# Another order of the prologue and the first phase in a hand-ordered fp32 attention block

## The reference, cut to what matters

```
x = x + 0.5 * ffn(_layernorm(x))       # ffn: layernorm with gamma, beta; times ternary weight; plus bias
x = x + attn(_layernorm(x))            # 16 query heads, 4 key/value heads, head size 128, rope
x = x + 0.5 * ffn(_layernorm(x))       # the same ffn weights
...
allowed = (j <= i) & (i - j <= WINDOW)                   # WINDOW = 64
weights = softmax(where(allowed, q @ k.T / sqrt(HD), -inf))
...
scale = mean(abs(w)); w_q = clip(round(w / (scale + Q_EPS)), -1, 1)
```

## Time and profile before

| | us |
|---|---|
| median of 3 runs | 791.79 |
| the profiled execution | 793.39 |
| its span, first to last instruction | 790.5 |
| PE busy | 778.3 |
| DVE, ACT, POOL busy | 626.1, 469.6, 455.7 |

### The profile page before, as it was taken

How to read it: one execution, slowest core, us unless ns; L and a number is a source line. 1 busy time by engine, 2 the same in 40 slices (tenths; PEclk the granted TensorE clock), 3 DMA queues, 4 the chain that set the end, 5 groups by cost and what they waited for, 6 DMA issues and landing times.

```text
span 790.5 us, 16087 instructions
## 1 busy us (share of the span) xinstructions
PE 778.3 (98%) x5630; PEld 727.2 (92%) x5630; DVE 626.1 (79%) x1321; ACT 469.6 (59%) x1602; POOL 455.7 (58%) x466
## 2 busy tenths in 40 slices
PE   8999999999999999999999999999999999999997
PEld 7688999999999999999999999999999999999996
DVE  5888967988688877888769887688867988688757
ACT  5366665657646565655747556475664657645574
POOL 3778555766446754567536773476635676446443
PEclk9999999999999999999999999999999999999999
DMA  8572324352252423425153242533224452243410
GB/s 300 114 194 59 90 55 120 95 127 48 55 152 63 121 54 89 126 55 120 41 135 94 68 99 49 134 92 97 67 55 121 94 129 45 57 104 68 107 29 27
DMA packets 54352, 74.10 MB, mean 94 GB/s; under 512 B 7168, under 2 KB 30208, under 8 KB 54272
## 3 DMA queue, kind: packets, MB, share of 16 engines
q1 hardware_dynamic: 53712, 72.74, 37.7%
q10 hardware_dynamic: 560, 0.34, 0.2%
HBM read 14.33 MB, written 4.19 MB: 23 GB/s over the span
## 4 chain that ended last, share of the span: by engine, by line
PE 92%; DVE 3%; POOL 2%; DMA 1%; issue 1%; ACT 0%; SPq 0%; DVEq 0%; POOLq 0%
PE job_p L656 33%; PE attn_p L656 22%; PE scores_p L673 13%; PE heads_p L656 11%; PE probsT_p L737 7%; PE job_p L833 4%; PE job_p L817 2%; POOL q_s L1282 1%; DMA x_res<-wo 1%; POOL probs L1271 1%; DMA x_in<-x 0%; DVE parts L1015 0%; DMA rope_swap<-rope_sin 0%; POOL wo_s L1253 0%; DVE rope_sin L934 0%
## 5 line engine op out<-in xcount | busy, mean ns | idle before, releaser
L656 PE MATMUL attn_p<-wo_s,headsT 128*128 128x256 f32 x1536 | 209.2, 286 | 1.0 <-ACT headsT L1175 0.7
L656 PE MATMUL job_p<-xnT,wq_s 128*128 128x512 f32 x768 | 205.3, 403 | 1.2 <-DVE v_s L951 1.1
L656 PEld LDWEIGHTS attn_p<-wo_s,headsT 128*128 128x128 f32 x1536 | 196.5, 191 | 7.0 <-ACT headsT L1175 1.4
L1154 ACT ACTIVATE probs<-scores_p,neg_max 128x96 f32<-128x96 f32 x512 | 167.6, 352 | 51.8 <-DVE neg_max L900 51.6
L1271 POOL TENSOR_TENSOR probs<-probs,inv_sum 128x384 f32<-128x384 f32 x128 | 107.9, 843 | 152.0 <-DVE inv_sum L906 151.9
L1282 POOL TENSOR_TENSOR q_s<-q_s,rope_swap 128x512 f32<-128x512 f32 x128 | 164.3, 1291 | 52.3 <-DMA rope_swap<-rope_sin 52.2
L1175 ACT ACTIVATE headsT<-heads_p,columns_s 128x512 fp32r<-128x512 f32 x128 | 88.0, 688 | 140.9 <-PE heads_p L656 140.5
L656 PEld LDWEIGHTS job_p<-xnT,wq_s 128*128 128x128 f32 x768 | 135.8, 189 | 26.6 <-DVE v_s L951 1.7
L934 DVE SCALAR_TENSOR_TENSOR rope_sin<-job_p,columns_s,rope_t 128x512 f32<-128x512 f32 x160 | 118.9, 743 | 21.1 <-PE job_p L656 19.9
L673 PE MATMUL scores_p<-k_s,q_s 128*128 128x96 f32 (+2 forms) x1024 | 131.6, 272 | 0.3 <-POOL q_s L1282 0.2
L673 PEld LDWEIGHTS scores_p<-k_s,q_s 128*128 128x128 f32 x1024 | 126.5, 192 | 3.4 <-POOL q_s L1282 1.1
(11 more groups left out here) (96 smaller groups left out, 972.7 us busy)
## 6 DMA issues: line engine op xcount, KB each, us to landing
rope_swap<-rope_sin SPq DMA_DIRECT2D x320, 128.0 KB, 2.3
v_odd<-v_s SPq DMA_DIRECT2D x64, 192.0 KB, 3.3
x_in<-x SPq DMA_DIRECT2D x15, 256.0 KB, 4.2
out<-x_res SPq DMA_DIRECT2D x15, 256.0 KB, 2.5
x_tr<-x_transposed SPq DMA_DIRECT2D x7, 512.0 KB, 5.3
q_s<-wq SPq DMA_DIRECT2D x3, 512.0 KB, 10.1
q_s<-wo SPq DMA_DIRECT2D x2, 512.0 KB, 10.6
x_res<-wo SPq DMA_DIRECT2D x2, 512.0 KB, 4.8
```

Source lines behind the costliest of these rows:

```text
L656: mm = nc.tensor.matmul(dst, a(p), b(q), start=clears and i == 0, stop=len(pairs) == 1, skip_group_check=True)
L1154: ins = nc.scalar.activation(probs[:, i, k, 0:REACH], scores_p[i][:, k, 0:REACH], ACT.Exp, bias=neg_max[:, i, k:k + 1], accum_out=row_sum[ ...
```

## The change

Only the orders and the counts of the fills change; no operation is rewritten. In the prologue, VectorE issues `ones` after the statistics of half 0, and `YT1` after half 0's second statistics; PE's orders of YT, FO, XT and V follow half 0 first, then half 1. The value job V10 moves from the first phase into the prologue on PE, ACT and DVE. The low part of w1 moves from VectorE to GpSimd (w0's is there already). SP issues the load for w11 (`stage8`) after Q1's swap, no longer after Q3's, and in the first phase `loadt0n` comes after Q7's swap and `stage9` after Q4's. ACT splits w11 ahead of exp0 and w9 behind it. The fills are 12, 2, 1, 2 and 5, in the order 0, 4, 2, 1, 3, before 10, 2, 1, 3 and 3 in the order 0 to 4. The tables of the middle and the last phase stay.

```diff
--- before.py
+++ after.py
@@ -59,17 +59,17 @@
 
 TENSOR = {
     "prologue": """
-        fill0i total0i fill1i YT0n YT1n beta0i FO0n gsum0i fill2i FO1n open0i fill3i XT0n fill4i
-        XT1n V00n K0n Q0n Q1n Q2n V01n Q3n
+        fill0i total0i fill4i YT0n fill2i beta0i FO0n YT1n open0i FO1n gsum0i XT0n fill1i V00n
+        XT1n V10n K0n Q0n Q1n Q2n V01n Q3n fill3i
     """,
     "first": """
-        K1c Q4c Q5c S0c S1c Q6c V10c T0c Q7c W0c T1c S2c S3c O0c
-        K2c W1c Q8c Q9c T2c V11c S4c O1c W2c T3c Q10c O2c S5c W3c
-        T4c S6c Q11c K3c O3c W4c T5c S7c O4c Q12c W5c T6c S8c FO0n
-        O5c Q13c W6c T7c Q14c S9c O6c FO1n W7c Q15c XT0n T8c O7c S10c
-        W8c T9c S11c XT1n O8c K0n W9c V00n T10c Q0n O9c S12c W10c Q1n
-        T11c S13c O10c Q2n W11c T12c S14c O11c W12c T13c S15c V01n Q3n O12c
-        W13c T14c
+        K1c Q4c Q5c S0c S1c Q6c Q7c T0c K2c S2c W0c T1c S3c Q8c
+        O0c W1c Q9c T2c O1c S4c W2c T3c S5c V11c Q10c O2c W3c T4c
+        S6c Q11c K3c O3c W4c T5c S7c Q12c O4c W5c FO0n T6c S8c Q13c
+        O5c W6c Q14c T7c S9c O6c W7c FO1n T8c Q15c XT0n O7c W8c S10c
+        T9c XT1n S11c O8c K0n V00n W9c T10c S12c O9c Q0n W10c T11c S13c
+        O10c Q1n W11c T12c S14c Q2n O11c W12c T13c S15c Q3n V01n O12c W13c
+        T14c
     """,
     "middle": """
         K1c Q4c S0c Q5c O13p W14p T15p S1c V10c O14p W15p Q6c T0c Q7c
@@ -95,17 +95,17 @@
 }
 VECTOR = {
     "prologue": """
-        ones0i stats0n stats1n tern0i YT0n bias0n beta0i FO0n YT1n astats0n FO1n astats1n gsum0i anorm1n
-        w4i w2i XT0n w5i XT1n V00n K0n Q0n Q1n Q2n w1i V01n Q3n
+        stats0n ones0i stats1n tern0i YT0n bias0n beta0i FO0n astats0n YT1n FO1n astats1n XT0n w4i
+        anorm1n V00n w5i w2i gsum0i XT1n V10n K0n Q0n Q1n Q2n V01n Q3n
     """,
     "first": """
-        K1c Q4c Q5c max0c max1c inv0c Q6c inv1c w11f probsT0c Q7c heads0c max2c V10c
-        inv2c max3c probsT1c K2c heads1c Q8c inv3c stats0n probsT2c max4c Q9c heads2c inv4c Q10c
-        probsT3c stats1n V11c max5c probsT4c heads3c inv5c max6c Q11c inv6c w12f YT0n heads4c probsT5c
-        K3c max7c Q12c heads5c probsT6c max8c inv7c YT1n FO0n astats0n heads6c inv8c Q13c Q14c
-        probsT7c max9c FO1n heads7c astats1n probsT8c inv9c Q15c XT0n max10c heads8c XT1n probsT9c inv10c
-        max11c K0n heads9c inv11c V00n probsT10c heads10c max12c Q0n max13c inv12c probsT11c Q1n heads11c
-        inv13c probsT12c max14c Q2n heads12c inv14c probsT13c max15c Q3n V01n inv15c
+        K1c Q4c w11f max0c Q5c max1c inv0c Q6c inv1c Q7c probsT0c max2c max3c heads0c
+        inv2c probsT1c K2c inv3c Q8c heads1c probsT2c stats0n max4c stats1n Q9c probsT3c inv4c max5c
+        heads2c V11c Q10c inv5c YT0n max6c Q11c heads3c inv6c probsT4c w12f heads4c probsT5c K3c
+        Q12c max7c heads5c YT1n max8c inv7c probsT6c FO0n inv8c Q13c astats0n heads6c probsT7c Q14c
+        max9c FO1n heads7c astats1n probsT8c inv9c Q15c max10c XT0n heads8c max11c XT1n probsT9c inv10c
+        K0n heads9c max12c inv11c probsT10c Q0n heads10c V00n max13c inv12c probsT11c Q1n max14c inv13c
+        heads11c probsT12c Q2n inv14c probsT13c max15c heads12c Q3n inv15c V01n
     """,
     "middle": """
         heads13p K1c probsT14p max0c Q4c Q5c max1c heads14p evac0p inv0c probsT15p stats0p V10c inv1c
@@ -133,16 +133,16 @@
 }
 SCALAR = {
     "prologue": """
-        abs0i gamma0i norm0n norm1n YT0n w0i YT1n w2i w4i w5i anorm0n w6i XT0n w3i
-        mask0n XT1n mask1n V00n w1i w8i w7i V01n
+        abs0i norm0n gamma0i norm1n YT0n w0i w3i w1i YT1n w4i mask0n anorm0n mask1n XT0n
+        w5i V00n XT1n w2i w6i V10n w8i V01n w7i
     """,
     "first": """
-        w9f w11f exp0c exp1c mask2c mask3c probsT0c heads0c V10c probsT1c exp2c heads1c exp3c probsT2c
-        mask4c w10f mask5c V11c heads2c exp4c probsT3c mask6c YT0n YT1n w12f probsT4c heads3c exp5c
-        exp6c mask7c heads4c probsT5c mask8c probsT6c heads5c exp7c mask9c exp8c heads6c probsT7c anorm0n heads7c
-        exp9c mask10c probsT8c mask11c XT0n anorm1n heads8c probsT9c XT1n exp10c exp11c heads9c V00n mask12c
-        probsT10c mask13c heads10c probsT11c exp12c mask14c exp13c mask15c heads11c probsT12c heads12c probsT13c exp14c mask0n
-        V01n exp15c mask1n heads13c
+        w11f exp0c w9f exp1c mask2c probsT0c mask3c w10f exp2c heads0c probsT1c exp3c mask4c heads1c
+        probsT2c mask5c probsT3c heads2c exp4c V11c mask6c YT0n exp5c probsT4c mask7c heads3c w12f exp6c
+        heads4c probsT5c YT1n heads5c mask8c exp7c probsT6c exp8c heads6c mask9c probsT7c heads7c anorm0n probsT8c
+        exp9c mask10c XT0n anorm1n mask11c heads8c XT1n exp10c mask12c probsT9c exp11c heads9c V00n mask13c
+        probsT10c heads10c probsT11c exp12c exp13c mask14c mask15c probsT12c heads11c exp14c mask0n probsT13c heads12c exp15c
+        V01n mask1n heads13c
     """,
     "middle": """
         probsT14p heads14p probsT15p exp0c exp1c V10c heads15p probsT0c mask2c norm0p mask3c YT0p exp2c heads0c
@@ -166,14 +166,14 @@
 }
 GPSIMD = {
     "prologue": """
-        scale0n scale1n w0i bias1n ascale0n ascale1n w3i w8i w6i K0n Q0n Q1n Q2n Q3n
-        pad0i
+        scale0n scale1n w0i bias1n ascale0n w1i ascale1n w3i w6i w8i pad0i K0n Q0n Q1n
+        Q2n Q3n
     """,
     "first": """
-        w7f probs0c probs1c K1c Q4c Q5c Q6c Q7c probs2c w9f K2c scale0n probs3c w10f
-        Q8c probs4c Q9c bias0n Q10c scale1n probs5c probs6c offset0n Q11c center0n residual0c probs7c offset1n
-        ascale0n bias1n center1n probs8c K3c Q12c ascale1n probs9c probs10c Q13c Q14c Q15c K0n probs11c
-        probs12c probs13c Q0n Q1n probs14c Q2n probs15c Q3n
+        w7f probs0c K1c probs1c Q4c w9f Q5c Q6c probs2c Q7c probs3c w10f K2c scale0n
+        Q8c probs4c bias0n probs5c Q9c Q10c probs6c Q11c scale1n offset0n residual0c center0n bias1n probs7c
+        probs8c offset1n ascale0n center1n K3c Q12c ascale1n probs9c Q13c Q14c Q15c probs10c probs11c probs12c
+        probs13c K0n probs14c Q0n Q1n Q2n probs15c Q3n
     """,
     "middle": """
         K1c Q4c probs0c scale0p probs1c Q5c Q6c scale1p Q7c probs2c bias1p bias0p probs3c scale0n
@@ -192,11 +192,11 @@
 }
 SYNC = {
     "prologue": """
-        K0n Q0n Q1n Q2n Q3n stage8i shift0n
+        K0n Q0n Q1n stage8i Q2n Q3n shift0n
     """,
     "first": """
-        loadt0n K1c Q4c Q5c Q6c load0n Q7c K2c stage9f Q8c Q9c Q10c Q11c K3c
-        Q12c shift1c Q13c Q14c Q15c K0n Q0n Q1n Q2n Q3n shift0n
+        K1c Q4c stage9f Q5c Q6c Q7c loadt0n load0n K2c Q8c Q9c Q10c Q11c shift1c
+        K3c Q12c Q13c Q14c Q15c K0n Q0n Q1n Q2n Q3n shift0n
     """,
     "middle": """
         K1c loadt0n Q4c Q5c Q6c load0n Q7c K2c Q8c Q9c Q10c store0p Q11c store1p
@@ -212,7 +212,7 @@
 }
 
 
-FILLS = (10, 2, 1, 3, 3)
+FILLS = (12, 2, 1, 2, 5)
 PARTS = {"p": -1, "c": 0, "n": 1}
 WAVES = ("YT", "FO", "stats", "scale", "norm", "bias")
```

## The result

The changed kernel takes 795.75 us (median of 6 runs, 794.57 to 796.89), the kernel before 791.78 in 6 runs beside it: a ratio of 1.0041, 95% interval 1.0026 to 1.0056, 3.3 us slower by the ratio. I forecast 791.7 with 789.7 to 793.6: the forecast was no change, the result is slower, outside the range. The profiled execution took 796.26 us with a span of 794.5, 4.0 us more than before.

A forecast was written before the change was run, and what follows sets the result against it. TensorE, busy 778.3 of 790.5 us, was taken as the bound, so the time PE reaches O3 decides. +3.5 - 0.4 - 3.15 = -0.05 us gave 791.7 us, range 789.7 to 793.6.

The forecast's parts named there:

- Part A: Up to K0: late `ones` and fills, V10 done there already; K0 at 26.3 us against 22.84, +3.5 us.
- the 0.53: PE's idle us ahead of T0, from ScalarE's split of w11 waiting for its load; claimed to go.
- so GpSimd is no bound: Between K0 and S0: GpSimd's queue runs to about 31.2 us, when K0's swapped half has only landed.
- part B: K0 to S0: w1's low part leaving DVE counts 0.3, K0's successor takes 0.1 less; -0.4 us.
- part C: S0 to O3: PE loses V10's 1.45 us and some idle time; 29.4 us against 32.56, -3.15 us.
- the slower one: Rival: the clock rises so late that `total`, `fill4` and YT0 also run at half speed; 793.7 us, chance 0.18.
- behind O3: Stretch from 70.05 to 783 us: pure PE work, tables untouched, passing earlier gains or losses on unchanged.
- the scaling at 55.26: DVE's scaling of two numbers, 1.48 us beside GpSimd's split; expected again, 0.8 to 0.9 us late, passed to Q10.
- the wait of 1.09: PE's idle us ahead of the Q job at 67.19 us; its cause was expected to come back, 0.8 to 0.9 us.

The follow-up runs named there:

- experiment 7: The kernel of experiment 6 with the value job V10 back in the first phase on PE, DVE and ACT; ratio 0.9981 to the kernel before.
- experiment 6: Changed kernel with w11's load ahead of K0's swap, Q9's products ahead of batch 1's statistics, `ones` ahead of half 0's statistics; ratio 0.9957, 788.63 us.
- experiment 4: The kernel before with one step moved: VectorE sets `ones` behind the statistics of half 0; ratio 1.0006 to the kernel before.
- experiment 1: The changed kernel with SP issuing w11's load ahead of K0's swap; ratio 1.0014 to the kernel before.
- experiments 5: The kernel of experiment 1 with Q9's two products ahead of batch 1's statistics on VectorE; ratio 0.9993 to the kernel before.
- experiment 3: The changed kernel with VectorE setting `ones` ahead of the statistics of half 0; ratio 1.0034 to the kernel before, runs from 792.4 to 798.6 us.

## Why the prediction was wrong

**Part A held in its size.** `ones` at 5.2 and fills to 10.2, FO0's addition at 14.76 (forecast 15.2), XT1's low part over at 25.55 (25.8), K0 at 25.6 (26.3). That the first fills run at the lower level of 1.2 GHz stands on their length alone, 0.20 us each on average here against 0.11 later: the granted clock of this stretch is shown as 1.00. One link was read wrongly: I had V10's last products end at 26.3, held back by XT1's low part. V10 needs half 0 alone and was over by 25.2, and K0 stands right behind XT1's low part, since it uses XT1's bank. That V10 fits in and pays back held too (experiment 7). What the late `ones` costs depends on the orders around it: 3.3 us at K0 and 2.9 us in all in the mended orders (experiment 6), 0.3 us at K0 in those of before (experiment 4).

**The step that failed** is the sentence on the moved load: "The load now goes out after Q1's swap; it lands before the scores are there, and the 0.53 goes." True, and it counts only what waits for the load. The load was moved past the swaps of Q2 and Q3 on SP's queue and on the DMA engines, and this I priced at nothing. With it fails "so GpSimd is no bound" of part B, which looks at K0's swap alone. Q2's copies took 4.7 us to land instead of 2.3, GpSimd came to Q3's addition 1.0 us late and so ran into VectorE's split of w11, for another 0.95 us. That is 2.0 us ahead of S0 (experiment 1 removes both). Part B was -0.4 and came out as +1.8.

**The second miss hangs on the first.** In part C I took the clock as granted throughout. The 2.03 us of idle time were followed by 3.4 us at half clock, 1.6 us of PE's time, and part C came out as -1.3 instead of -3.15. None of my rivals had this place: the slower one put a low clock at the fills, where it stayed a matter of tenths. The whole account, forecast against measured: part A 0.7 us less, part B 2.2 more, part C 1.9 more (1.6 of it the clock), behind O3 0.7 more, together 4.1 on a forecast of -0.05. That A's error and the rest behind O3 cancel is chance. Nor do the 3.6 us of waiting and clock all come back when the load is moved: experiment 1 gained 2.2.

**What came back as expected, though I had read its cause from the wrong row**: a scaling held up beside GpSimd. I named the scaling at 55.26, 11 us ahead of the wait of 1.09. Right ahead of that wait stand the operations of half 1; the one behind its scaling is held up beside an addition on GpSimd (65.26 to 66.52):

```profile
65.24 1.31 DVE L1026 TENSOR_SCALAR minus_mean<-stats 128x2 f32<-128x2 f32 x1
```

The changed kernel has 0.81 us at 61.05, beside an addition that ends at 61.83, and not the over 1 us beside a split that I had as a sign. Experiment 1 has 1.65 us from 58.34: GpSimd's split ends at 58.73 and the addition behind it at 59.96, so the scaling waited through both. PE waits 1.10 and 1.93 us ahead of Q10; forecast 0.9. The Trainium skill (SBUF — State Buffer, "Who interferes with whom") has the later of the two wait for the whole instruction of the other. By that rule, the trace agrees in the changed kernel: 61.05 + 0.81 is 61.86.

## What to carry to other kernels

A step that is moved up a queue has two prices: that of its own late or early result, and that of everything which now stands behind it. Here a 512 KB load ahead of the short copies of a swap made them land after 4.7 us instead of 2.3. Put such a load where the queue is idle (here 9 us ahead of the first swap). Look also at which long operations of VectorE and GpSimd meet: whether w11's split or Q3's addition came first, a matter of 0.2 us, decided over 0.95 us of PE's wait. And an idle time of 2 us ahead of matmuls may cost nearly as much again by the clock behind it. A delay of the first fills was nearly free in one order of the prologue and cost 3 us in another.

## What I had not expected

The clock makes the value of one step depend on its surroundings: `ones` late costs 0.0006 of the time in the kernel before (within the noise), 0.0036 between experiments 5 and 6. And kernels whose idle time lies at such a place seem to spread (I didn't test the cause): 6 us between ten runs in experiment 3, while five of the six runs of experiment 6 lie within 0.3 us.
